# Weights loaded a stage ahead, and in the state space two of sixteen C products moved to GpSimd, the skip term to TensorE and the gate product to VectorE

## The reference, cut to what matters

```python
xn = layernorm(x) * ln_w + ln_b
x_inner, z = split(xn @ W_in.T)                    # 256 channels each
u = silu(causal_conv4(x_inner, conv_w) + conv_b)
dt_low, B, C = split(u @ W_x.T, [64, 80])          # B, C: 16 states
dt = clip(softplus(dt_low @ W_dt.T + b_dt) + 0.001, 0.001, 0.1)
A = -exp(log_A)
h_t = exp(dt_t * A) * h_(t-1) + (dt_t * u_t) * B_t # for each channel and state
y_t = sum over the 16 states of h_t * C_t
y = (y + u * D_param) * silu(z)
x = y @ W_out.T + x
```

## Time and profile before

| | before |
|---|---|
| median of 3 runs | 4124.1 us (4123.56 to 4127.41) |
| profiled execution, its own time | 4123.32 us |
| its span | 4121.5 us |
| busy in the span: TensorE | 3433.0 us (83%) |
| VectorE | 2923.0 us (71%) |
| ScalarE | 1910.0 us (46%) |
| GpSimd | 1529.9 us (37%) |
| mean granted TensorE clock | 0.925 of full speed |

### The profile page before, as it was taken

One profiled execution on the slowest core, in us unless ns is written; L12 is line 12 of the kernel. 1 busy time (PEld: TensorE's weight loads), 2 busy tenths in 40 slices (PEclk: granted clock), 3 DMA queues, 4 the chain that ended last, 5 costly groups with the idle time before them and its releaser, 6 DMA issues. The chain is left out here.

```text
span 4121.5 us, 60315 instructions
## 1 busy us (share of the span) xinstructions
PE 3433.0 (83%) x20989; PEld 2119.0 (51%) x21044; DVE 2923.0 (71%) x6308; ACT 1910.0 (46%) x3495; POOL 1529.9 (37%) x1002
## 2 busy tenths in 40 slices
PE   5999998969999962877558888888877999999767
PEld 3767675647777752544323333333334666666423
DVE  7888887557777736333259999999995666666575
ACT  2655565225556520322146666666652222232365
POOL 2311111631121101788647777877860000000062
PEclk9999999989999965999879999999998999999868
DMA  6333331024444340333322222222213222222101
GB/s 150 89 90 88 92 87 35 1 51 104 102 102 101 86 132 11 43 43 43 73 69 67 76 69 62 78 67 62 80 54 106 92 93 90 92 91 93 54 1 42
DMA packets 238095, 305.25 MB, mean 74 GB/s; under 512 B 45986, under 2 KB 157315, under 8 KB 227540
## 3 DMA queue, kind: packets, MB, share of 16 engines
q1 hardware_dynamic: 203876, 280.11, 24.8%
q0 software_dynamic: 22528, 17.32, 3.2%
q10 hardware_dynamic: 11392, 3.97, 0.5%
HBM read 243.54 MB, written 56.56 MB: 73 GB/s over the span
## 5 line engine op out<-in xcount | busy, mean ns | idle before, releaser
L574 DVE TENSOR_REDUCE a_Mx<-a_Sx 128x2 f32<-128x512 f32 (+1 forms) x1024 | 590.5, 618 | 173.0 <-PE a_Sx L626 126.7
L2163 POOL TENSOR_TENSOR a_inp<-a_dtu,a_Bs 128x1024 f32<-128x1024 f32 x256 | 605.1, 2385 | 94.9 <-DVE a_h L2327 93.7
L2327 DVE TENSOR_TENSOR_SCAN a_h<-a_dA,a_inp 128x1024 f32<-128x1024 f32 x256 | 584.3, 2282 | 5.3 <-ACT a_dA L2255 5.3
L2417 PE MATMUL a_Y<-a_hc,g_ident 128*128 128x512 f32 x1024 | 520.8, 634 | 8.1 <-DVE a_hc L2337 8.0
L347 POOL TENSOR_TENSOR a_rest<-a_qk,a_parts 128x512 f32<-128x512 f32 x64 | 75.3, 1177 | 917.5 <-ACT a_parts L399 917.5
L2255 ACT ACTIVATE a_dA<-a_dtA,a_A 128x512 f32<-128x512 f32 x512 | 331.3, 682 | 174.6 <-DVE a_h L2327 173.9
L413 ACT ACTIVATE a_Pr<-a_SA 128x512 f32<-128x512 f32 x512 | 305.1, 596 | 167.9 <-DVE a_SA L524 79.3
L623 PE MATMUL a_Sx<-att_Kp,att_Qp 96*128 96x256 bf16 (+1 forms) x2048 | 347.2, 262 | 41.6 <-DMA att_Qp<-a_crows 18.5
L1990 ACT ACTIVATE f_sg<-f_GB 128x512 f32<-128x512 f32 x272 | 162.6, 598 | 470.2 <-PE f_GB L2039 470.0
L2066 PEld LDWEIGHTS f_OUT<-f_wd,f_hm 128*128 128x128 f32 x2176 | 284.2, 191 | 139.5 <-issue 112.6
L1957 DVE TENSOR_TENSOR f_sg<-f_sg,f_UB 128x512 f32<-128x512 f32 x256 | 175.9, 687 | 232.7 <-PE f_UB L2041 210.2
(11 more groups left out here) (441 smaller groups left out, 7007.6 us busy)
## 6 DMA issues: line engine op xcount, KB each, us to landing
a_Bs<-a_brows SPq DMA_DIRECT2D x256, 256.0 KB, 3.3
f_Cs<-f_crows SPq DMA_DIRECT2D x512, 128.0 KB, 2.9
att_Qp<-a_packing SPq DMA_DIRECT2D x192, 192.0 KB
att_Kp<-a_packing SPq DMA_DIRECT2D x192, 192.0 KB
a_packing<-a_parts SPq DMA_DIRECT2D x64, 384.0 KB, 2.8
a_packing<-a_parts SPq DMA_DIRECT2D x64, 128.0 KB, 2.8
g_x<-x SPq DMA_DIRECT2D x8, 512.0 KB, 7.3
f_sum<-g_x SPq DMA_DIRECT2D x1, 4096.0 KB, 13.1
```

The costliest lines, as they stand in the source:

```text
L574: nc.vector.tensor_reduce(Mx[(k + 2 - (j < LATE)) % 2][:, t, 2 * jj:2 * jj + 2], Sx[t][:, 0:2 * wd].rearrange("p (h q) -> p h q", h=2), AX ...
L2163: nc.gpsimd.tensor_tensor(inp[n % Q][:], dtu[k][:], Bs[n % Q][:].unsqueeze(1).to_broadcast([P, CH, GT]), ALU.mult).then_inc(s["mulB"], 1)
L2327: nc.vector.tensor_tensor_scan(h[n % 2][:].rearrange("p c q -> p (c q)"), dA[m % 2][:].rearrange("p c q -> p (c q)"), inp[n % Q][:].rearra ...
L2417: nc.tensor.matmul(Y[c][:], ident[:], hc[n % Q][:, c], start=(n == 0), stop=(n == N - 1))\
```

## The change

1. Loads. A helper `held_weights` keeps weights in the outermost scope, and each stage loads those of the next: experts those of the state space, the state space those of the routed experts (one load at the start of groups 1 to 6), the routed experts those of the GRU. In the router only three small constants stand ahead of the row stores; the copy of x and the large weights are issued behind them (`late_loads`).
2. From experts to state space. x comes back in five parts (4, 12, 16, 16, 16 tiles) whose semaphores outlive the block. The statistics and the factors move into the state space's block: tiles 0 to 3 first, then all others; `norm_factors` is not called. Group 0's front is written out (`first`), with several PSUM banks in place of the one `M`.
3. In the loop. C products of n = 2 and n = 5 run on GpSimd (`mulC`), from rows of C that SyncE spreads from DRAM. The skip term u D becomes a matmul with a diagonal (`diag`) that opens the sum in `Y`. VectorE multiplies Y by the gate directly. The cap moves from VectorE to GpSimd, the shift of dt by 0.001 to ScalarE (Identity with a bias); the clip from below is done by the cap. The split of B and C needs two GpSimd instructions and one ScalarE copy. VectorE's residual add and statistics move from n = 15 to behind scan 0 of the group after.

```diff
@@ expert_choice, router_scores, choose
-        def loads(sp):
+        def loads(sp):
+            for dst, src in ((same, "same"), (prior, "before"), (tcol, "tcol")):
+                sp.dma_start(dst[:], w[src]).then_inc(small, 16)
+
+        def late_loads(sp):
             sp.dma_start(sum_v, x[:]).then_inc(copied, 16)
             for dst, src in ((w1, "w1"), (w2, "w2"), (b1, "b1"), (b2, "b2"), (iota, "iota"), (slot, "slot")):
                 sp.dma_start(dst[:], w[src]).then_inc(big, 16)
...
+            for g in range(GROUPS):
+                wait(sp, xn_ready, G * (g + 1))
+                sp.dma_start(keep[:, G * g:G * g + G, 0:D], xn[g % NX][:]).then_inc(kept[g % NX], 16)
+            late_loads(sp)
...
+                load_next(sp)
                 for i in range(NY):
                     sp.wait_ge(added[i], 64 * len(range(i, GROUPS_E, NY)))
-                for i in range(8):
-                    sp.dma_start(x[:, 8 * i:8 * i + 8], sum_v[:, 8 * i:8 * i + 8]).then_inc(back[i], 16)
+                for lo, hi, back in res["back"]:
+                    sp.dma_start(x[:, lo:hi], sum_v[:, lo:hi]).then_inc(back, 16)
...
-                for i in range(8):
-                    v.wait_ge(back[i], 16)
-                    for t in range(8 * i, 8 * i + 8):
-                        nc.vector.bn_stats(res["stats"][:, t, :], x[:, t, :])
@@ routed_experts, min_gru: the loads at the start become
-            for dst, n in loads:
-                sp.dma_start(dst[:], w[n]).then_inc(s["loaded"], 16)
-            for dst, n in ((wg, "wg"), (wu, "wu"), (wd, "wd")):
-                sp.dma_start(dst[:], w[n]).then_inc(s["weights"], 16)
+            load_next(sp)
@@ state_space, SyncE
+                if 1 <= g <= 6:
+                    load_next(sp, g - 1)
...
+                    if on(1) and n == N - 2:
+                        wait(sp, s["mulC_pool"], len(MOVED) * (g + 1))
+                        for i, nn in enumerate(MOVED):
+                            sp.dma_start(Cs[i][:], bass.AP(brows.tensor, ((k + 1) % 2 * 2 * N + N + nn) * GT,
+                                                           [[0, P], [1, GT]])).then_inc(s["c_in"], 16)
@@ state_space, GpSimd
+            def mulC(m, n):
+
+                wait(pool, s["c_in"], 16 * len(MOVED) * (m // N + 1))
+                wait(pool, s["scanned"], m + 1)
+                wait(pool, s["y_mm"], CH * (m + 1 - Q))
+                C = Cs[MOVED.index(n)][:].unsqueeze(1).to_broadcast([P, CH, GT])
+                nc.gpsimd.tensor_tensor(hc[n % Q][:], h[n % 2][:], C, ALU.mult).then_inc(s["mulC_pool"], 1)
...
+                    if n - 1 in MOVED and on(0):
+                        mulC(g * N + n - 1, n - 1)
+                    if on(1) and n == 10:
+                        rest_of_rows(g + 1, (k + 1) % 2)
+                    if on(1) and n == 12:
+                        last_rows(g + 1, (k + 1) % 2)
+                    if on(1) and n == 11 and g >= 0:
+                        cap(g + 1)
+                    if on(1) and n == 13 and g >= 0:
                         steps(g + 1, (k + 1) % 2)
@@ state_space, ScalarE
                     nc.scalar.activation(et[:], et[:], ACT.Ln, bias=1.0).then_inc(s["ln_done"], 1)
+                    wait(act, s["ln_done"], b + 1)
+                    wait(act, s["scanned"], N * (b - 1))
+                    nc.scalar.activation(dtA[j][:], et[:], ACT.Identity, bias=least[:]).then_inc(s["dt_done"], 1)
@@ state_space, VectorE
                     for c in range(CH):
-                        nc.vector.scalar_tensor_tensor(out=yy[:, c], in0=u[k][:, c], scalar=dpar[:, c:c + 1],
-                                                       in1=Y[c][:], op0=ALU.mult, op1=ALU.add).then_inc(s["y_read"], 1)
-                if n == 15:
+                        nc.vector.tensor_tensor(yy[:, c], Y[c][:], sz[k][:, c], ALU.mult).then_inc(s["y_read"], 1)
+                if n == N:
...
+                    if on(-2) and n == 0:
+                        finish(g - 2, k, N)
                     if on(-1):
                         finish(g - 1, (k + 1) % 2, n)
-                    if on(0):
-                        wait(v, s["cc_mm"], m + 1)
+                    if on(0) and n not in MOVED:
+                        wait(v, s["cc_mm"], by_vector(m))
@@ state_space, TensorE
                         if n == 0:
                             wait(pe, s["y_read"], CH * g)
-                        wait(pe, s["mulC"], g * N + n + 1)
+                            for c in range(CH):
+                                nc.tensor.matmul(Y[c][:], diag[:, c], u[k][:, c], start=True, stop=False)
+                        wait_product(pe, g * N + n)
```

More of the change, by code:

```diff
@@ L1678, in choose @@
         sc = Scope(nc, ctx, name + "c")
-        same, before = sc.sb("same", [P, P]), sc.sb("before", [P, P])
+        same, before, tcol, loaded = held
         s, junk, eq, pre = (sc.sb(n, [P, BL, P]) for n in ("s", "junk", "eq", "pre"))
@@ L2125, in _, with by_vector, by_pool, wait_product @@
+        def by_vector(m):
+            return m // N * (N - len(MOVED)) + sum(n not in MOVED for n in range(m % N + 1))
+        def by_pool(m):
+            return m // N * len(MOVED) + sum(n in MOVED for n in range(m % N + 1))
+        def wait_product(eng, m):
+            if m >= 0 and m % N in MOVED:
+                wait(eng, s["mulC_pool"], by_pool(m))
+            elif m >= 0:
+                wait(eng, s["mulC"], by_vector(m))
         @block.sync
         def _(sp):
-            for dst, n in loads:
-                sp.dma_start(dst[:], w[n]).then_inc(s["loaded"], 16)
@@ L2198, in front, with first_gate @@
+            def first_gate():
+                wait(act, s["m_read"], U)
+                nc.scalar.activation(sz[0][:], sz[0][:], ACT.Silu).then_inc(s["sz_ready"], 1)
             def front(g, k, n):
@@ new lines, in _, with first @@
+            for part, (lo, hi, back) in enumerate(res["back"]):
+                v.wait_ge(back, 16)
+                for t in range(lo, hi):
+                    last = nc.vector.bn_stats(stats[:, t, :], x[:, t, :])
+                then(last)
+                if part == 0:
+                    factors(0, 0, G)
+            factors(1, G, TILES)
+            def first():
+                wait(v, s["m_read"], ET_FIRST)
+                nc.vector.tensor_scalar(et[:], et[:], CAP, 0.0, ALU.min, ALU.max).then_inc(s["capped"], 1)
+                wait(v, s["dt_done"], 1)
+                wait(v, s["u_ready"], 1)
+                nc.vector.tensor_tensor(dtu[0][:], dtA[0][:], u[0][:], ALU.mult).then_inc(s["dtu_done"], 1)
+                wait(v, s["dtu_done"], 1)
+                nc.vector.memset(dtA[0][:].rearrange("p c (b s) -> p (c b) s", b=NB)[:, :, 0:1], 1e25)\
+                    .then_inc(s["dt_ready"], 1)
@@ L2424, in state_constants @@
     sel = np.zeros((P, 32, P), HOST_BF16)
-    for r in range(96):
+    for r in (*range(32), *range(64, P)):
         sel[r, r % 32] = 1.0
@@ L2542, in layout @@
     low[:, :, 0:64] = wx[:, :, 0:64]
-    for r in range(3):
+    for r in (0, 2, 3):
         bcs[:, :, 32 * r:32 * r + 32] = wx[:, :, 64:96]
```

356 lines of the change are left out of this document (227 added, 129 removed).

## The result

The changed kernel takes 4055.95 us (median of 4 runs, 4053.43 to 4057.97) against 4125.76 us for the kernel before beside it: a ratio of 0.983, 95% interval 0.9813 to 0.9847. It is faster, by 70 us or 1.7%, where 105 us were forecast; 4056 lies just outside the range of 3984 to 4052. A later series of 4 runs gave 4053.23 against 4123.51, ratio 0.9835 (0.9819 to 0.9852). The profiled execution has a span of 4056.1, 65.4 under that of before.

The account below looks back on a forecast made before the run. VectorE was taken to set the state space's pace. Router 19.4, entry 29.6, loop and end 47.6 and later stages 8.4 sum to 105.0; 4124.1 - 105.0 = 4019 us, range 3984 to 4052.

Parts of the forecast that it names:

- Router: In the router, the fifth normalization no longer waits for row stores queued behind large loads: minus 19.4 us.
- Entry: From the copy back of x to the state space's first scan: minus 29.6 us, rough by 8 either way.
- (a): First stretch of the state space's entry, from the copy back of x to group 0's normalization: 11.2 us.
- (b): Second stretch of the state space's entry, to the first product with the low-rank weights: 17.7 us, gaining 24.0.
- (c): Third stretch of the state space's entry, to the first scan: 15.9 us for 21.5 before, gaining 5.6.
- The loop, VectorE's side: In the state space's loop, VectorE's work and waits shrink by 5.2 us a group, to an interval of 56.2.
- What may be late next: In the loop, VectorE waits per group 1.15 us for ScalarE and 1.2 for TensorE; GpSimd fits; 2.85 gain remains.
- ScalarE at the end: At a group's end, one more ScalarE pass of 1.06 us makes the next group's scan 0 late by 1.15.
- it fits on average: In the loop, GpSimd's work was summed to 49.7 us of a 56.2 group, so it would fit.
- Scans wait for GpSimd: In the state space's loop, a stated sign that the prediction is wrong; no size given.
- the loop gains nothing: Rival: GpSimd and VectorE hold each other up, or GpSimd falls behind at group's end; 44 us back, 4063; chance 0.12.
- Later stages: Routed experts and GRU get their weights during the stage before: 2.84 and 5.52 us, minus 8.4 in all.

Follow-up runs that it names:

- e2: Changed kernel without the diagonal matmuls, so the output lacks the skip term: group 59.17 us against 60.87, total 4043.2 us beside 4142.7 for the kernel before.
- e7: Changed kernel with the diagonal matmuls at step 14 instead of the group's start: group 59.05 us, total 4035.6 us beside 4123.3 for the kernel before.
- e6: Changed kernel with GpSimd taking C products 6 and 8 instead of 2 and 5: group 61.32 us, total 4063.3 us beside 4123.3 for the kernel before.
- e3: Changed kernel with only the shift of dt folded into the logarithm: group 60.65 us, total 4053.8 us beside 4123.3 for the kernel before.
- e4: Changed kernel with only the row store moved behind the load of B row 12: group 60.62 us, total 4052.2 us beside 4123.3 for before.
- e5: Changed kernel with the edits of e3 and e4 together: group 59.32 us, total 4043.6 us beside 4142.7 for the kernel before.
- e12: Changed kernel with diagonal matmuls at step 14 and all C products on VectorE: group 60.55 us, total 4068.1 us beside 4132.8 for before.
- e11_weights_later: Changed kernel with the state space's weight loads issued behind the experts' first scatter: group 60.90 us, total 4070.1 us beside 4132.8 for before.

## Why the prediction was wrong, step by step

*Router: right.* The wait of 19.4 is gone, and the first gather starts 18.1 earlier (1611.44 against 1629.57); 0.9 was already lost ahead of the router, whose first normalization starts that much later (1473.78 against 1472.84).

*State weights during the experts: right,* nothing, by the spread above.

*Entry: nearly.* From the copy back to the first scan 48.6 for 44.9 forecast, 25.8 gained for 29.6. Stretch (a) took 12.7 for 11.2: the next block's first work comes at 2031.3, 4.0 after SyncE's last issue, where 1.3 had been read off the end of a block that VectorE ended. (b) took 18.3 for 17.7. (c) took 17.6 for 15.9: the product with the low-rank weights ran at 3.78 against 1.98, at a granted clock of 0.50 (the 1.2 GHz level) behind an idle stretch, and the first scan waited 3.39 for GpSimd. In the other runs the same stretch takes 47.7 to 51.2, so its parts are sure to a few us only.

*The loop, VectorE's side: right.* 56.2 was forecast without waits; 60.87 - 4.53 = 56.3 was measured.

*What may be late next: here it failed.* Forecast were two waits, 1.15 + 1.2 = 2.35; there are 4.53. That makes 2.2 x 14 = 31 of the 35 us that the loop and its end fell short; the other 4 lie in the first and last groups and weren't broken down. The three parts of the step:

- TensorE: mis-sized. The step had one set of four passes at the low clock, plus 1.7. The trace has two, the diagonals and the first sum, plus 2.8 in the group shown and 2.35 on average (3.52 and 2.59 for 1.88), since the change itself put a set in front. From the end of product 0 to product 6 TensorE's chain takes 19.5 on average for the 18.7 forecast, and VectorE's own work there 17.1 for 17.4, so the wait up to product 6 is 2.4 for 1.2. It is met in pieces, at products 3 (0.9) and 4, at scan 6 and at product 6 (1.05); since TensorE never pauses, these pieces are parts of one lateness and not additions to it. Product 7, which the forecast didn't look at, adds 0.2: 2.7 in all. e2 and e7 show that the chain's length is the cause.
- ScalarE at the end: 1.4 at scan 0 for 1.15, nearly right in size, though GpSimd holds the scan as long. But scan 9, behind ScalarE's SiLU of u, was not looked at: 0.34, and 1.65 with the moved products at 6 and 8 (e6).
- GpSimd: "it fits on average" hid that it sits idle 10.66 before its multiply 12 and is just as late as ScalarE at scan 0. SyncE's order had the store of the rows ahead of B row 12 already in the kernel before; there GpSimd did four passes of 1.15 over the rows in that gap. The forecast counted its work and not what each piece waits for. e3, e4 and e5 show it. It cost nothing beside ScalarE's wait, but makes a repair of either one alone look useless. The cap, taken at 2.4 after a two-input multiply of the same shape, lasts 1.04, so GpSimd's sum of 49.7 was too high (47.1) and GpSimd was late all the same. "Scans wait for GpSimd" was one of the stated signs of being wrong, and they do, 16.6 in the loop.

*The rivals.* The total (4056) lies between the forecast and "the loop gains nothing" (4063), and the group of 60.87 is close to the one near 61 that was to mean the latter. That the total came near this rival's is no support for its first cause, engines that hold each other up: that is refuted. Its second, GpSimd behind at the group's end, is there, but costs nothing beside ScalarE's wait of the same length. The Trainium skill (Perfetto Trace Analysis, Optimizing Scalar/DVE Operations) warns that work moved between VectorE and GpSimd may not help, since they share a port. The Trainium skill (GPSIMD Engine Reference, Specifications) narrows this to VectorE instructions in a two-port mode or with two SBUF inputs. The trace agrees with the narrower one as far as it goes (the loop has no VectorE instruction with two SBUF inputs, so what one would do isn't shown): the scan and the product each have one of their two inputs in PSUM, GpSimd is busy in 5.74 of a stretch of 6.40, and scan, product and GpSimd's multiply keep their durations (2284, 1221, 2360 ns). The outcome of the rule, little gained by the moved products, came by another mechanism, and with the diagonals late more of it is gained (1.50 of 2.44, e12 and e7).

*Later stages: right,* 8.6 for 8.4, with 1.1 more by the end.

## What to carry to other kernels

When work leaves the engine that sets the pace, don't compare the sums of the others with the new pace: take each in-order engine from the point where it last stood idle, write down when each of its deliveries is ready, and compare with the new demand at every delivery: the largest lateness counts, and the waits on the way to it are parts of it. Added work belongs where its engine has slack (the diagonals cost 1.8 a group at step 0 and nothing at step 14), and work is best taken from the bound engine behind the last delivery that comes late (product 9 instead of 5). If two repairs at one wait give nothing each (60.65 and 60.62 for 60.61, and 59.32 together), try them together before dropping them.

## What the runs showed of the hardware

TensorE, back from an idle stretch of 5.40 (changed kernel) or 4.48 (e7), ran its first set of four passes in 3.62 in the groups shown, diagonals or sums alike, for 1.88 later. In the changed kernel the granted clock over these first 6.40 was 0.54, mostly the 1.2 GHz level. A second set directly behind took 2.91 in the group shown and 1.88 to 2.96 over the twelve, 2.59 on average.

In the changed kernel, where the experts' stage ends with SyncE's copies, the next stage's first work starts 4.0 after SyncE's last issue; in the kernel before, where VectorE ends that stage, it starts 1.3 after VectorE's last work. What the 4.0 consist of isn't shown.

GpSimd's cap, one input of 128x1024 in float32, took 1.04; its multiply of two inputs of that shape 2.36.

On two of the four occasions the experts took 10 to 13 longer from the first gather to the first scatter (38.9 to 41.5 for 27.7 to 29.8), and one chip showed both. The kernel before took 4142.7 and 4132.8 on these two, 19 and 9 more than on the others, but has no trace there. TensorE in e11_weights_later, in order of time, stands in the middle of them with no semaphore that the profile could name:

```profile
1631.73 1.10 PE L1564 MATMUL f3e_U<-f3e_xnT,f_w 128*128 128x512 f32 x2 [3.41 <-issue]
```

What it waits for there is open; no run was made for it.
